# Order of the last part of a transformer layer's kernel: four context products and a second correlation ahead of the loop, statistics one tile at a time, and another order on GpSimd

## The reference

```python
x = x + attn(layernorm(x), ...)            # 4-bit weights, low-rank adapters, gated feed-forward
x = x + autocorrelation(layernorm(x), ctx, ctx)
x = x + routed_adapters(layernorm(x), route_w, A, Bw)
```

```python
corr = ifft(fft(q) * conj(fft(k))).real    # 64 lags
w, idx = top_k(corr, 8); w = softmax(w)
out = sum_i w[i] * v[min(idx[i] + pos, 63)]
...
logits = x @ route_w.T                      # 8 experts, the best one
out = (one_hot(best) * logit * (x @ A)) @ Bw
```

## Time and profile before

| | us |
|---|---|
| median of 3 runs | 814.45 (813.24 to 821.21) |
| the profiled execution | 818.46 |
| its span in the trace | 816.2 |
| PE busy | 764.9 (94%) |
| DVE busy | 571.7 (70%) |
| ACT, POOL busy | 411.4, 243.4 |

### The profile page before, as it was taken

The page is one execution under the profiler, slowest core; times in us unless marked ns, Lnnn a source line. Parts: engine busy times, 40 slices in busy tenths (PEclk is TensorE's granted clock), DMA queues, the critical chain, the costliest instruction groups (busy, mean ns, idle before and its releaser), DMA issues.

```text
span 816.2 us, 10572 instructions
## 1 busy us (share of the span) xinstructions
PE 764.9 (94%) x3384; PEld 553.3 (68%) x3384; DVE 571.7 (70%) x1291; ACT 411.4 (50%) x743; POOL 243.4 (30%) x196
## 2 busy tenths in 40 slices
PE   3979999999999999999999999999997989999975
PEld 1335778778888888888888888887774545455532
DVE  5997874667897377567647738652347799999983
ACT  7784743565755355355344535521124456666541
POOL 0001221023453342342433334231111433333341
PEclk9999999999999999999999999999999799999997
DMA  7374210012323022112203201120250554556401
GB/s 220 133 257 127 68 52 1 1 39 67 114 78 104 14 89 79 39 39 85 84 14 103 79 14 65 39 73 1 64 127 8 126 143 117 147 145 156 123 26 39
DMA packets 31285, 67.26 MB, mean 82 GB/s; under 512 B 4800, under 2 KB 5184, under 8 KB 31232
## 3 DMA queue, kind: packets, MB, share of 16 engines
q1 hardware_dynamic: 31232, 66.60, 28.1%
HBM read 45.61 MB, written 4.19 MB: 61 GB/s over the span
## 4 chain that ended last, share of the span: by engine, by line
PE 67%; DVE 24%; issue 3%; ACT 3%; DMA 1%; POOL 1%; SPq 0%; DVEq 0%; POOLq 0%; ACTq 0%
PE ps L666 19%; PE ps L668 19%; PE ps L667 19%; DVE mark L1021 3%; DVE pp L976 2%; DVE wl L1064 2%; DVE top L1000 2%; PE ps L896 1%; DVE pc L1097 1%; DVE st L836 1%; PE ps L637 1%; DVE fin L1206 1%; DVE stats L535 1%; DVE x L1128 1%; PE ps L1119 1%
## 5 line engine op out<-in xcount | busy, mean ns | idle before, releaser
L666 PE MATMUL ps<-x_hi,w_hi 128*128 128x512 f32 x448 | 176.2, 393 | 0.1
L668 PE MATMUL ps<-x_hi,w_lo 128*128 128x512 f32 x448 | 174.7, 390 | 0.0
L667 PE MATMUL ps<-x_lo,w_hi 128*128 128x512 f32 x448 | 174.4, 389 | 0.0
L782 POOL TENSOR_TENSOR h_lo<-hf,h_hi 128x512 fp32r<-128x512 f32 x56 | 74.0, 1321 | 244.5 <-ACT h_hi L777 244.4
L791 DVE TENSOR_TENSOR acc<-acc,ps 128x512 f32<-128x512 f32 x112 | 76.3, 684 | 73.4 <-PE ps L668 73.4
L770 DVE TENSOR_TENSOR hf<-hf,ps 128x512 f32<-128x512 f32 x56 | 38.4, 686 | 87.0 <-PE ps L668 87.0
L666 PEld LDWEIGHTS ps<-x_hi,w_hi 128*128 128x128 f32 x448 | 84.1, 188 | 21.6 <-issue 4.0
L523 POOL TENSOR_TENSOR w_lo<-wt,w_hi 128x512 fp32r<-128x512 f32 x42 | 62.4, 1486 | 113.8 <-ACT w_hi L516 113.8
L668 PEld LDWEIGHTS ps<-x_hi,w_lo 128*128 128x128 f32 x448 | 84.1, 188 | 18.0
L667 PEld LDWEIGHTS ps<-x_lo,w_hi 128*128 128x128 f32 x448 | 84.2, 188 | 17.3
L666 PE MATMUL ps<-w_hi,h_hi 128*128 128x512 f32 x224 | 87.9, 392 | 1.9 <-DVE acc L717 1.4
(11 more groups left out here) (150 smaller groups left out, 1349.3 us busy)
## 6 DMA issues: line engine op xcount, KB each, us to landing
codes_sb<-in_codes SPq DMA_DIRECT2D x40, 256.0 KB, 3.0
scale_sb<-in_scale_rows SPq DMA_DIRECT2D x80, 128.0 KB, 2.9
kc<-ku SPq DMA_DIRECT2D x64, 128.0 KB, 2.4
kx<-ku SPq DMA_DIRECT2D x32, 256.0 KB, 3.8
lft<-in_lora_ft SPq DMA_DIRECT2D x14, 512.0 KB, 4.2
acc<-in_x SPq DMA_DIRECT2D x4, 1024.0 KB, 8.4
ctx<-in_ctx SPq DMA_DIRECT2D x16, 256.0 KB, 3.9
out<-fin SPq DMA_DIRECT2D x16, 256.0 KB, 3.8
```

The lines of the kernel that those rows point to most:

```text
L666: nc.tensor.matmul(bank, hi, rhs_hi, start=start, stop=False)
L667: nc.tensor.matmul(bank, hi, rhs_lo, start=False, stop=False)
L668: return nc.tensor.matmul(bank, lo, rhs_hi, start=False, stop=stop)
L782: nc.gpsimd.tensor_tensor(h_lo[:, c % 2, i], hf[:, i], h_hi[:, c % 2, i].bitcast(F32), ALU.subtract).then_inc(hlo_done, 1)
```

## The change

It reorders; no arithmetic changes. One ring (ku) gets a sixth buffer. Ahead of the loop now stand context product 3 (`pe_ku`, `act_ku`, `sp_spread`), tile 1's `dve_product` and `pe_corr`, and tile 0's `pe_w` and `act_w`; within the drain the additions go between these. The third and fourth chunks' `x_stats` are cut into `x_stat` (one BN_STATS) in slots 1 to 8 and `x_mean` in 4 and 8; `x_rstd` goes to slots 5 and 9. On GpSimd, `pool_cross` of a tile comes ahead of `pool_divide` of the next, and on DVE `dve_weigh` comes behind the first half of `dve_mark`.

```diff
-    KU_RING, KX = 5, 4
+    KU_RING, KX = 6, 4
...
-        for s in range(SUB):
-            nc.vector.bn_stats(stats[:, s], acc[:, SUB * (c % NCH) + s]).then_inc(ln1, 1)
+        nc.vector.bn_stats(stats[:, s], acc[:, SUB * (c % NCH) + s]).then_inc(ln1, 1)
+
+    def x_mean(dve, c):
...
-    wide = [(FORWARD, 0), (FORWARD, 1), (FORWARD, 2), (QUERY, 0)]
+    wide = [(FORWARD, 0), (FORWARD, 1), (FORWARD, 2), (QUERY, 0), (FORWARD, 3), (BACKWARD, 0)]
...
-    LATER = (1, 5)
+    LATER = (3, 7)
...
             def piece(at):
+                if a := at(2):
+                    pool_cross(pool, *a[:2])
+                if a := at(1, 1):
+                    pool_divide(pool, *a[:2])
+                if a := at(2):
+                    pool_pow(pool, *a[:2])
                 if (a := at(1)) and a[0] in LATER:
                     x_pow(pool, NCH + 2 + a[0] // 4)
-                if a := at(2):
-                    pool_cross(pool, *a[:2])
-                if a := at(2):
-                    pool_pow(pool, *a[:2])
-                if a := at(0, 1):
-                    pool_divide(pool, *a[:2])
...
+            act_ku(act, 3)
+            act_normalise_x2(act, 2, 0)
             act_exp_top(act, 0, 0)
             act_exp(act, 0, 0)
             act_lags(act, 0, 0)
+            act_w(act, 0, 0)
...
             dve_less(dve, 0, 0)
             dve_negate(dve, 0, 0)
+            dve_add(dve, NG - 1, NCH - 1, 0)
             for half in range(2):
                 dve_mark(dve, 0, 0, half)
+            dve_add(dve, NG - 1, NCH - 1, 1)
             dve_sum(dve, 0, 0)
             dve_invert(dve, 0, 0)
-            dve_add(dve, NG - 1, NCH - 1, 0)
-            dve_add(dve, NG - 1, NCH - 1, 1)
+            dve_product(dve, 1, 1)
+            dve_add(dve, NG - 1, NCH - 1, 2)
             dve_weigh(dve, 0, 0)
-            dve_add(dve, NG - 1, NCH - 1, 2)
             dve_add(dve, NG - 1, NCH - 1, 3)
...
-                if a := at(0, 1):
+                if a := at(0, 2):
                     dve_product(dve, *a[:2])
...
-                if (a := at(0)) and a[0] in LATER:
-                    x_stats(dve, NCH + 2 + a[0] // 4)
+                if (a := at(1)) and a[0] < SUB:
+                    x_stat(dve, NCH + 2, a[0])
+                if (a := at(2)) and SUB - 1 <= a[0] < 2 * SUB - 1:
+                    x_stat(dve, NCH + 3, a[0] - SUB + 1)
+                if (a := at(1)) and a[0] in LATER:
+                    x_mean(dve, NCH + 2 + a[0] // 4)
...
+                if a := at(0, 1):
+                    dve_mark(dve, *a[:2], 0)
                 if a := at(1, 1):
                     dve_weigh(dve, *a[:2])
-                if a := at(0, 1):
-                    dve_mark(dve, *a[:2], 0)
...
                         pe_corr(pe, 0, 0)
+                        pe_ku(pe, 3, 1, 1)
                     pe_down(pe, *last, 3)
...
             pe_down(pe, NG - 1, 0, NCH - 1, 2)
+            pe_down(pe, NG - 1, 0, NCH - 1, 3)
+            pe_corr(pe, 1, 1)
             pe_lags(pe, 0, 0)
-            pe_down(pe, NG - 1, 0, NCH - 1, 3)
+            pe_w(pe, 0, 0)
```

More of the change, by code:

```diff
@@ L524, in pool_lo, with x_stat @@
                                 ALU.subtract).then_inc(lo_done, 1)
-    def x_stats(dve, c):
-        n = LNS * c
+    def x_stat(dve, c, s):
         if c < NCH:
@@ L533, in x_stats @@
             dve.wait_ge(added, 4 * (NCH * (NG - 2) + c + 1))
-        for s in range(SUB):
-            nc.vector.bn_stats(stats[:, s], acc[:, SUB * (c % NCH) + s]).then_inc(ln1, 1)
+        nc.vector.bn_stats(stats[:, s], acc[:, SUB * (c % NCH) + s]).then_inc(ln1, 1)
+    def x_mean(dve, c):
+        n = LNS * c
         if real(n):
@@ L544, in x_stats @@
         nc.vector.tensor_scalar(ve[:], mv[:, :, 1], EPS, None, ALU.add).then_inc(ln1, 1)
+    def x_stats(dve, c):
+        for s in range(SUB):
+            x_stat(dve, c, s)
+        x_mean(dve, c)
     LNS = 2 * SUB + 5
@@ L923, in build @@
     emptied = (ku_copied, psame, prod, lag_copied, h_copied, fin_done, x3_done)
-    wide = [(FORWARD, 0), (FORWARD, 1), (FORWARD, 2), (QUERY, 0)]
+    wide = [(FORWARD, 0), (FORWARD, 1), (FORWARD, 2), (QUERY, 0), (FORWARD, 3), (BACKWARD, 0)]
     for v in range(TT + 4):
-        wide += [(BACKWARD, v - 2)] * (0 <= v - 2 < TT) + [(FORWARD, v + 2)] * (3 <= v + 2 < TT)
+        wide += [(BACKWARD, v - 2)] * (1 <= v - 2 < TT) + [(FORWARD, v + 2)] * (4 <= v + 2 < TT)
     query = []
@@ L1271, in _ @@
                 sp_ctx(sp, t, t)
-            for t in range(3):
+            for t in range(4):
                 sp_spread(sp, t, t % 2)
@@ L1278, in piece @@
                     sp_store(sp, *a[:2])
-                if a := at(-2, 3):
+                if a := at(-2, 4):
                     sp_spread(sp, *a[:2])
-                if a := at(-4, 5):
+                if a := at(-4, 6):
                     sp_ctx(sp, *a[:2])
@@ L1471, in piece @@
                     act_normalise_x3(act, *a[:2])
-                if a := at(-2, 2):
+                if a := at(-2, 3):
                     act_normalise_x2(act, *a[:2])
@@ L1485, in piece @@
                     act_exp(act, *a[:2])
-                if a := at(1):
+                if a := at(1, 1):
                     act_w(act, *a[:2])
@@ L1779, in piece @@
                     pe_q(pe, *a[:2])
-                if a := at(2):
+                if a := at(2, 1):
                     pe_w(pe, *a[:2])
```

## The result

| | before | after |
|---|---|---|
| median of 20 runs, us | 817.73 (813.24 to 822.88) | 815.35 (808.94 to 817.45) |
| ratio after / before | | 0.9964 (95% interval 0.9948 to 0.9981) |
| profiled execution, us | 818.46 | 815.15 |
| its span, us | 816.2 | 813.0 |

What follows compares the result with a forecast made beforehand. DVE was taken to set the even slot's pace, with PE next at about 10.0 us. Terms -2.5 + 0 - 0.4 - 0.9 + 0.4 + 1.4 - 2.5 - 1.0 = -5.5 us gave 809.0 from 814.45; range 800.5 to 815.5.

Steps and rivals of the forecast that it cites:

- the even slot: Loop: wl falls to 0.67, DVE's slot by 0.85 to 9.69; PE then bounds at about 10.0, saving 0.5 a slot.
- the term of slots 10 to 14: Five even slots in the loop, each 0.5 us shorter: -2.5 us in all.
- The steps of x_rstd: Slots 5 and 9: pn holds steps by 2.1 and 1.5, clock costs 1.2 in slot 5 only; slots -0.4 and +1.4.
- The mean's addition: Slots 4 and 8: one-input addition might lose up to about 1.2 us each to pn; not in the sum.
- The start: Drain ahead of the loop: -2.5 us at the second correlation, low clock assumed again; ends -6 and 0.
- A: Slots 5 and 9: no x_rstd step held, no low clock in slot 5; -10.3, 804.2 us; chance 0.28.
- B: Slots 10 to 16: even slot stays since DVE waits for the gather or en; -2.0, 812.4 us; chance 0.14.
- C: GpSimd's pn starts before nm, holding it and four steps 1.1 us a slot; +13.2, 822.2 us; chance 0.08.
- slot 15 and the next: End of the loop: the even slot's 0.5 us saving in each of these two, -1.0 us in all.

Runs made afterwards that it cites:

- wl's place alone: Kernel before with one edit, wl moved behind the first half of the marks; ratio 0.9924 (0.9900 to 0.9948).
- the run with GpSimd's old order: Changed kernel with en again ahead of pn and the chunk's power between the divide and pn of the slot before; ratio 0.9869 (0.9846 to 0.9892).
- the one in which pn waits: Changed kernel with pn waiting for nm of the tile behind it and, in slots 5 and 9, x_rstd's last step; ratio 0.9866, span 804.4.
- the run with x_rstd behind wl: Changed kernel with x_rstd's four steps, and in slot 5 the BN_STATS following them, moved behind wl; ratio 0.9947, span 808.2.
- start alone: Kernel before with only the change's drain, ring and prologue; ratio 1.0006 (0.9987 to 1.0026).
- statistics: Kernel before with only one BN_STATS a slot, means in slots 4 and 8, x_rstd in slots 5 and 9; ratio 0.9981 (0.9952 to 1.0011).
- the run with 10 products: Changed kernel with 10 products of constants, results unused, on PE behind the correlation in slots 5 and 9; ratio 0.9882 (0.9857 to 0.9908).

## Why the prediction was right or wrong

- **What bounds, and the even slot: right.** wl's 0.85 and the hand-over to PE at about 10.0 were read from the rows; it is 9.89, and the term of slots 10 to 14 was -2.5 and measured -3.15. I credited it to the wrong edit, though. I took GpSimd's order to be what frees wl. wl's place alone does it, because half of the marks is just enough for the old pn to end.
- **The steps of x_rstd: the right mechanism, too small.** This is the step that failed: "I take 2.1 for slot 5 and 1.5 for slot 9 ..., in slot 9 I take none" for the clock. Slot 9 measured +5.0 against my +1.4, slot 5 +1.2 against -0.4. These two terms were 5.2 us short. Both slots lost 2.15 to the holds (slot 5 had the same 1.28 and 1.19), for which I had 2.1 and 1.5: that was right in one and 0.6 short in the other. For the idle PE and its clock I had 1.2 and nothing, and each slot lost 2.8 to them, of which an estimated 2.2 to 2.7 are the clock. So 4.4 of the 5.2 are this one term. I had seen that PE would idle behind the steps in slot 5, and had written it off in slot 9 without working out its idle time, which was 1.94.
- **The mean's addition.** I put no price on it in the sum. The rule that I cited from the Trainium skill (SBUF — State Buffer, Who interferes with whom), by which a `tensor_scalar` can be held too, holds here: it took 0.64 and 0.68 us beside pn in slots 4 and 8, and 0.17 where GpSimd is idle. That is 0.5 a slot: from pp to pc DVE took 4.02 and 4.06 in these two slots, and 3.54 in both in the run with GpSimd's old order, where the addition ran free. With it slots 3, 4 and 8 gave +1.2 in place of +0.4.

```profile
649.85 2.51 POOL L1112 TENSOR_TENSOR pn<-wu,kx 128x512 f32<-128x512 f32 x2 [1.47 <-ACT wu L1097]
...
650.51 0.64 DVE L545 TENSOR_SCALAR ve<-mv 128x4 f32<-128x4 f32 x1
```

- **The start: right in kind, mis-sized.** -2.5 was forecast and -6.07 measured in the profile. The low clock did come behind the idle 2.84 us that I had worked out, but it was over sooner: the second correlation (tile 2's) took 2.11 us and not 3.65, and the gathers were half done at full clock.

```profile
629.57 2.11 PE L993 MATMUL ps<-spec,pp 128*128 128x64 f32 x16 [2.84 <-ACT ex L1043]
```

  I had that as the term's other end, -6. It isn't luck of this one profile alone: of the six runs that have the changed kernel's start and statistics as they are, five have product 3 at 34.1 to 34.2 behind product 0, and the one in which pn waits at 35.8. The 3.6 more than forecast hid part of the miss of the two slots; without it the profile of the changed kernel would have come out no faster. That the total was off by 2.6 us only is therefore luck: two misses of opposite sign.
- **The rivals.** A (nothing held) fell by the 1.28 and 1.19. B (the even slot stays) fell. C, pn ahead of nm, did not occur in the changed kernel. It did in the run with x_rstd behind wl, at a lead of 0.04 us and in two slots, 6 and 10; it did not feed itself, as the slots after them were 10.37 and 9.99. The last tiles saved 0.4 where I had 1.0 for slot 15 and the next.

Together: by themselves the change's parts are worth 0 (start alone), 0.2% (statistics; neither is clear of the noise) and 0.8% (wl's place), and GpSimd's order takes back about 1%: the changed kernel is at 0.9964 with it and at 0.9869 without. On the kernel before with wl's place it takes back 0.7% (0.9924 to 0.9995).

Left open: why the clock's low stretch is long in one execution and short in another, or stays away behind the same idle time. The times of one kernel vary by 1% with the mean clock of the run (0.976 to 0.986 after the change), and I did not find what sets it.

## What to carry to other kernels

Before moving an instruction of GpSimd, list the small instructions of VectorE that read two tiles in on-chip memory and can meet it; each can lose most of one instruction of GpSimd (1.1 us here), at a lead of hundredths of a microsecond. Order them by a semaphore, not by hope: the wait that let pn start 0.6 later paid 1% here. And price a stall that leaves TensorE idle for about 2 us at its own length plus the slower products behind it; here that doubled it (2.15 us of holds, and some 2.2 to 2.7 of slower clock).

## What the runs showed of the hardware that I had not expected

- Starting together (707.13 both, and 662.90 both) the VectorE step passed, in the run with 10 products; 0.01 us later (709.34 against 709.33, and 661.22 against 661.21) it lost 1.1 us, in the changed kernel.
- Cheap products whose results nobody reads paid for themselves: 2.4 us of them on TensorE's queue in each of two slots made these 3.9 and 3.4 shorter, with a granted clock of 1.00 in place of 0.66 to 0.77. Some 1.0 of each is the hold that did not come about there, and no merit of theirs.
- The clock fell behind an idle time of 1.94 us in one place (slot 9) and stayed full behind 1.91 in another: the idle time ahead of tile 1's correlation in the kernel before (1.00 in 620 to 630). Behind 1.61 and 1.62, at the same place of the tail, it stayed full in one run and fell in another.
